# A graph propagation and a set-choosing LSTM on one core: the last propagation pass written out by row block, the first input weights fetched earlier

## The reference, cut to what matters

```python
# x: (1250, 512) float32; 21250 edges (src, dst, edge_weight)
def gnn(x, alpha, beta, sigma, edge_val, edge_row, edge_col, num_iters=10):
    xn = x * rsqrt(max(sum(x*x, axis=1, keepdims=True), 1e-12))
    sim_e = sum(xn[edge_row] * xn[edge_col], axis=-1)      # 0 on the diagonal
    sup = edge_val * exp(sim_e / (4 * exp(sigma)**2))
    denom = b + segment_sum(sup, edge_row)[:, None] * a + a   # a, b = exp(alpha), exp(beta)
    out = x
    for _ in range(num_iters):                              # 10 passes
        Ax = segment_sum(sup[:, None] * out[edge_col], edge_row)
        out = (x * b + (Ax + out) * a) / denom
    return out

def lstm(x, W_ih, W_hh, b_ih, b_hh, W_sel, b_sel):          # 4 weight sets, 1250 steps
    for t in range(1, T):
        logits = concat(h, c, x[t]) @ W_sel.T + b_sel
        s = argmax(logits)                                  # the set of this step
        g = x[t] @ W_ih[s].T + h @ W_hh[s].T + b_ih[s] + b_hh[s]
        h, c = lstm_activate(g, c)

x = x + gnn(layernorm(x))          # x1 in the kernel
return x + lstm(layernorm(x))      # y in the kernel is layernorm(x1)
```

## Time and profile before

| what | before |
|---|---|
| three executions, us | 6814.09, 6814.86, 6822.49 (median 6814.86) |
| the profiled execution, us | 6817.24 |
| its span, us | 6815.5 |
| granted TensorE clock, mean | 0.959 of full speed |
| busy: TensorE matmul / weight load | 6117.3 us (90%) / 4119.5 us (60%) |
| busy: VectorE / ScalarE / GpSimd | 3616.7 (53%) / 1805.4 (26%) / 1686.4 (25%) |

### The profile page before, as it was taken

How to read it: one execution, slowest core, us unless ns; L and a number is a source line. 1 busy time by engine, 2 the same in 40 slices (tenths; PEclk the granted TensorE clock), 3 DMA queues, 4 the chain that set the end, 5 groups by cost and what they waited for, 6 DMA issues and landing times.

```text
span 6815.5 us, 340711 instructions
## 1 busy us (share of the span) xinstructions
PE 6117.3 (90%) x126674; PEld 4119.5 (60%) x126675; DVE 3616.7 (53%) x19152; ACT 1805.4 (26%) x6561; POOL 1686.4 (25%) x4128
## 2 busy tenths in 40 slices
PE   6727999789999999999999999999999999999986
PEld 3523444666666666666666666666666666666663
DVE  5553111245565556555665555566556655556555
ACT  1001000522332223223332333233333333233321
POOL 4733111412222222222222222222222222222220
PEclk8758999589999999999999999999999999999999
DMA  3230000622222122122222222222222222222210
GB/s 95 1 77 0 0 0 0 192 71 58 62 63 58 57 60 65 55 60 60 65 63 60 62 61 60 60 63 63 61 60 65 64 61 63 59 63 62 61 52 27
DMA packets 691011, 389.94 MB, mean 57 GB/s; under 512 B 47835, under 2 KB 670811, under 8 KB 690720
## 3 DMA queue, kind: packets, MB, share of 16 engines
q1 hardware_dynamic: 659746, 369.66, 18.5%
q0 software_dynamic: 24192, 0.10, 1.1%
q10 hardware_dynamic: 7038, 19.69, 0.9%
HBM read 370.96 MB, written 18.38 MB: 57 GB/s over the span
## 4 chain that ended last, share of the span: by engine, by line
PE 70%; DVE 6%; issue 5%; DMA 1%; DVEq 0%; SPq 0%; ACT 0%; POOL 0%; POOLq 0%
PE ps L1016 33%; PE ps L1078 15%; PE ps L1025 8%; PE ps L1009 5%; PE ps L1005 4%; DVE hsum L843 2%; PE ps L1002 2%; PE ps L991 1%; DVE osum L851 1%; DVE acts L861 1%; DVE gates L848 1%; DVE osum L854 1%; DMA wring<-in_w_ih 1%; DVE cprod L857 0%; PE ps L978 0%
## 5 line engine op out<-in xcount | busy, mean ns | idle before, releaser
L1016 PE MATMUL ps<-WH,hparts 128*2 128x384 f16 x49760 | 2303.0, 326 | 196.6 <-issue 176.1
L1016 PEld LDWEIGHTS ps<-WH,hparts 128*2 128x2 f16 x49760 | 1053.4, 83 | 1044.7 <-issue 292.9
L843 DVE TRANSPOSE_TENSOR_REDUCE hsum<-ps 128x12 f32<-128x384 f32 x1250 | 728.7, 583 | 1793.0 <-PE ps L1016 1788.0
L1078 PE MATMUL ps<-xcur,wcur 128*128 128x64 f32 x9728 | 1341.9, 281 | 85.7 <-issue 12.4
L1078 PEld LDWEIGHTS ps<-xcur,wcur 128*128 128x128 f32 x9728 | 1178.5, 191 | 273.3 <-issue 210.2
L454 POOL COPY xT<-hfull 128x4 f32 x1250 | 239.5, 192 | 3727.2 <-DVE hfull L872 3727.2
L470 POOL COPY wcur<-wring 128x512 f32<-128x512 f32 x1216 | 743.4, 611 | 445.1 <-ACT gxb L598 443.3
L1025 PEld LDWEIGHTS ps<-WH,hparts 128*2 128x2 f16 x40000 | 603.7, 83 | 352.7 <-issue 314.9
L1025 PE MATMUL ps<-WH,hparts 128*2 128x128 f16 x40000 | 781.2, 219 | 7.5
L583 ACT ACTIVATE gx_now<-gxb 128x16 f32 x1250 | 269.7, 216 | 1782.2 <-DVE pick L837 1707.1
L969 PE MATMUL ps<-O,Adj 128*128 128x512 f16 x3000 | 650.3, 380 | 77.2 <-DVEq L748 77.2
(11 more groups left out here) (147 smaller groups left out, 4983.8 us busy)
## 6 DMA issues: line engine op xcount, KB each, us to landing
wring<-in_w_ih SPq DMA_DIRECT2D x1280, 256.0 KB, 2.9
gxb<-in_w_hh ACTq DMA_DIRECT2D x32, 512.0 KB, 5.6
adjacency<-Adj SPq DMA_DIRECT2D x2, 6400.5 KB, 24.7
Adj<-adjacency SPq DMA_DIRECT2D x10, 640.0 KB, 7.5
sim<-adjacency SPq DMA_DIRECT2D x10, 640.0 KB, 6.3
adjacency<-total,where_ POOLq DMA_INDIRECT x168
x_rows<-X SPq DMA_DIRECT2D x1, 2560.0 KB, 8.7
wring<-x_rows SPq DMA_DIRECT2D x10, 256.0 KB, 3.5
```

Of the source, the lines that this page charges most:

```text
L843: dve.tensor_reduce(hsum[:, :], gate_ps.rearrange("p (c q) -> p c q", q=32), AX.X, ALU.add, apply_transpose=True).then_inc(turned, 1)
L1016: last = nc.tensor.matmul(gate_ps[32 * j:32 * j + 2, :], hparts[:, k, :], WH[:, s * KC + k, part, j, 0:3 * P], start=(k == 0 and part == 0 ...
L1078: last = nc.tensor.matmul(unit_ps, wcur[:, k, :], xcur[:, k, :], start=(k == 0), stop=(k == KC - 1))
```

## The change

Five things are changed. (1) The tenth pass is taken out of the loops: VectorE updates X and takes the statistics of each row block as it arrives, after row block 7 (EARLY = 8) it also scales, roots and normalises blocks 0 to 7, and after block 9 the last two; ScalarE and GpSimd no longer split the tenth result. (2) Transposes go by group of four row blocks first and by piece k second, in both places where they are used. (3) `sim` is placed first in the graph's memory and `wring` first in the LSTM's, so that wring lies over sim. (4) SyncE fetches the first four slices when the matrix is finished (`m_ready`), and issues the write of the guessed sets behind the loads of the fourth group. (5) VectorE prepares biases and scales before the guessed sets, and TensorE does not wait for `lx_ready` any more.

```diff
         with ExitStack() as graph:
+            sim = sb("sim", [P, 2, NP], f32, graph)
             X = sb("X", [P, RT, D], f32, graph)
...
-            sim = sb("sim", [P, 2, NP], f32, graph)
...
+        wring = sb("wring", [P, SUB, KC, P], f32)
         WH = sb("WH", [P, S * KC, 2, 4, D], f16)
         gxb = sb("gxb", [P, 2 * TB, UNITS], f32)
-        wring = sb("wring", [P, SUB, KC, P], f32)
...
+        EARLY = 8
...
-            sp.wait_ge(x1_ready, 1)
-            sp.dma_start(x1_dram.rearrange("(t p) d -> p t d", p=P), X[:, :, :]).then_inc(x1_out, 16)
-            sp.wait_ge(lx_ready, 1)
-            sp.dma_start(pick_dram.rearrange("(t p) -> p t", p=P), pick_t[:, :], allow_slow_non_contiguous=True).then_inc(lx_out, 16)
-            sp.wait_ge(x1_out, 16)
-            sp.wait_ge(graph_free, 1)
...
+            sp.wait_ge(m_ready, RT)
+            for k in range(KC):
+                load_slice(sp.snap(0), 0, k)
+            sp.wait_ge(x1_ready, 1)
+            sp.dma_start(x1_dram.rearrange("(t p) d -> p t d", p=P), X[:, :, :]).then_inc(x1_out, 16)
+            for g in range(1, G):
+                for k in range(KC):
+                    if k < KC - 1:
+                        sp.wait_ge(wring_free, g * (KC - 1) + k + 1)
+                    else:
+                        sp.wait_ge(proj_mm, g * SUB + SUB)
+                    load_slice(sp.snap(0), g, k)
+            sp.wait_ge(lx_ready, 1)
+            sp.dma_start(pick_dram.rearrange("(t p) -> p t", p=P), pick_t[:, :], allow_slow_non_contiguous=True).then_inc(lx_out, 16)
+            with sp.Fori(1, S) as q:
-            with sp.Fori(0, S) as q:
...
-            with pool.Fori(0, ITERS // 2) as i:
+            with pool.Fori(0, ITERS // 2 - 1) as i:
...
+            for r in range(RT):
+                low_part(O_parts[0], r, (ITERS - 1) * RT + r + 1)
...
-            with act.Fori(0, ITERS // 2) as i:
+            with act.Fori(0, ITERS // 2 - 1) as i:
...
-            take_root(3)
+            for r in range(RT):
+                high_part(O_parts[0], r, (ITERS - 1) * RT + r + 1)
+            take_root(3, 0, EARLY)
+            take_root(4, EARLY, RT)
...
+            def finished_rows(r):
+                dve.wait_ge(t_ready, ITERS * RT + r + 1)
                 link(dve.scalar_tensor_tensor(out=X[:, r, :], in0=T[:, r, :], scalar=float(2.0 ** -OS), in1=X[:, r, :],
                                               op0=ALU.mult, op1=ALU.add))
+                link(dve.bn_stats(stats[:, r, :], X[:, r, :]))
+            def normalised_rows(first, end):
+                layernorm_scale(first, end)
+                for r in range(first, end):
+                    dve.tensor_scalar(O1[:, r, :], X[:, r, :], mv[:, r, 0:1], rstd[:, r:r + 1], ALU.subtract, ALU.mult).then_inc(y_ready, 1)
+            with dve.Fori(0, ITERS - 1) as i:
+                for r in range(RT):
+                    next_rows(r, dve.snap(i * RT + (r + 1)))
+            dve.wait_ge(t_low, ITERS * RT)
+            for r in range(RT):
+                next_rows(r, (ITERS - 1) * RT + r + 1)
+                finished_rows(r)
+                if r == EARLY - 1:
+                    normalised_rows(0, EARLY)
             dve.sem_inc(x1_ready, 1)
-            layernorm_stats()
...
+            normalised_rows(EARLY, RT)
...
-            def transposes(src, first, ready, want):
-                for k in range(KC):
-                    for q, (r0, m) in enumerate(TQ):
-                        i = first + k * len(TQ) + q
+            def transposes(src, first, ready, banks_free):
+                for q, (r0, m) in enumerate(TQ):
+                    if q == 1:
+                        banks_free()
+                    for k in range(KC):
+                        i = first + q * KC + k
...
-            transposes(O1, NTQ, y_ready, 0)
+            transposes(O1, NTQ, y_ready, lambda: pe.wait_ge(t_ready, (ITERS + 1) * RT))
...
-            pe.wait_ge(lx_ready, 1)
```

More of the change, by code:

```diff
@@ L314, in load_unit, with load_slice @@
                              ).then_inc(wring_in[u], 16)
-            with sp.Fori(0, S) as q:
+            def load_slice(q, g, k):
+                sp.dma_start(wring[:, k, :, :].rearrange("p u n -> p (u n)"),
+                             w_ih[:, bass.ds(q, 1), order[g], k * D:(k + 1) * D].rearrange("p a n -> p (a n)")
+                             ).then_inc(wring_in[k], 16)
+            sp.wait_ge(m_ready, RT)
[13 more added lines that the diff above has]
+            with sp.Fori(1, S) as q:
                 for g in range(G):
@@ L499, in _, with take_root @@
             act.activation(ab[:, 2:3], scal_b[:, 2:3], ACT.Exp, scale=-2.0).then_inc(ab_ready, 1)
-            def take_root(n):
+            def take_root(n, first=0, end=RT):
                 act.wait_ge(square_ready, n)
-                act.activation(root[:, :], square[:, :], ACT.Sqrt).then_inc(root_ready, 1)
+                act.activation(root[:, first:end], square[:, first:end], ACT.Sqrt).then_inc(root_ready, 1)
             take_root(1)
@@ L635, in _, with inverse_root @@
             roots = [0]
-            def inverse_root(to):
+            def inverse_root(to, first=0, end=RT):
+                to_c, root_c, newton_c, square_c = (one[:, first:end] for one in (to, root, newton, square))
                 roots[0] += 1
@@ L641, in inverse_root, with layernorm_scale @@
                 dve.wait_ge(root_ready, roots[0])
[L642 to L646, removed]
+                link(dve.reciprocal(to_c, root_c))
+                link(dve.tensor_tensor(newton_c, to_c, to_c, ALU.mult))
+                link(dve.tensor_tensor(newton_c, newton_c, square_c, ALU.mult))
+                link(dve.tensor_scalar(newton_c, newton_c, -0.5, 1.5, ALU.mult, ALU.add))
+                link(dve.tensor_tensor(to_c, to_c, newton_c, ALU.mult))
+            def layernorm_scale(first=0, end=RT):
+                for r in range(first, end):
+                    dve.bn_aggr(mv[:, r, :], stats[:, r, :]).then_inc(v, 1)
+                    chain[0] += 1
+                dve.wait_ge(v, chain[0])
+                link(dve.tensor_scalar(square[:, first:end], mv[:, first:end, 1], EPS, None, ALU.add))
+                inverse_root(rstd, first, end)
             def layernorm_stats():
@@ L652, in layernorm_stats @@
                 dve.wait_ge(v, chain[0])
[L653 to L658, removed]
+                layernorm_scale()
             dve.wait_ge(x_in, 32)
@@ L748, in _ @@
             dve.sem_inc(prop_ready, 1)
[L750 to L757, removed]
@@ L758, in _, with next_rows @@
-            for r in range(RT):
+            def next_rows(r, n):
+                dve.wait_ge(prop_mm, n)
+                dve.scalar_tensor_tensor(out=T[:, r, :], in0=ps[:, r % 8, :], scalar=float(2.0 ** -MS), in1=XB[:, r, :],
+                                         op0=ALU.mult, op1=ALU.add).then_inc(t_ready, 1)
+            def finished_rows(r):
+                dve.wait_ge(t_ready, ITERS * RT + r + 1)
                 link(dve.scalar_tensor_tensor(out=X[:, r, :], in0=T[:, r, :], scalar=float(2.0 ** -OS), in1=X[:, r, :],
```

27 lines of the change are left out of this document (11 added, 16 removed).

## The result

| what | before | changed |
|---|---|---|
| six executions each, median us | 6817.83 | 6786.39 (6782.36 to 6793.79) |
| the profiled execution, span, us | 6815.5 | 6783.0 |
| granted TensorE clock, mean | 0.959 | 0.962 |

What follows compares the result with a forecast made beforehand. TensorE bounds 70% of the span; what matters is the stretch from last propagation matmul to first LSTM step. -41.2 + 11.5 + 1.2 - 1.5 = -30.0 us gives 6787.2 profiled, 6784.8 against the median; range 6770 to 6797.

Steps and rivals of the forecast that it cites:

- its own signs: Prediction wrong if block 9's row is over 6.5 us late, fifth-group stall absent or over 14 us, or LSTM time changes.
- End of propagation: VectorE's early part ends before block 9 arrives, so no delay; X complete at 1210.0, last normalisations at 1212.7 us.
- Transposes to logits: Most transposes and copies run before the last normalisations; graph_free at 1214.2 us, logits start 22.8 us earlier.
- Logits: The 80 set-logit matmuls on TensorE stay unchanged at 15.8 us.
- Logits to projection: Biases prepared earlier save 4.6 us, first slices fetched early 13.8; projection starts at 1231.9 us.
- The words: Writing the guessed sets' 1280 words ahead of the fifth group's refills stalls TensorE there, costing 11.5 us, bounds 0 and 14.
- Sharing with the recurrent weights: Projection groups sharing DMA with recurrent-weight loads take 7.69 us; 1.2 us lost, bounds 0 and 4.
- First transposes: Early in the kernel, the new order waits for four blocks instead of ten: 1.5 us earlier, bounds 0 and 1.7.
- A (no stall): Rival: SyncE's refills in projection aren't held by the words; gain 41.5 us, time 6773; chance 0.13.
- B: Rival: moved SBUF places cost in every LSTM step; break-even 24 ns per step, 6847 us at 50 ns; chance 0.05.
- C (full clock in projection): Rival: TensorE stays at clock 1.0 through logits and projection; logits 8 us less, time 6762; chance 0.06.
- D (gain given back): Rival: words stall projection refills twice, or sharing costs 8.4 us a group; 17 us more, 6802; chance 0.05.

Runs made afterwards that it cites:

- order-only kernel: Kernel before with only the new order of the transposes, in both places: 6810.6 us, ratio 0.9996.
- places-only: Kernel before with only the new places in SBUF (sim first in the graph's memory, wring first in the LSTM's): 6818.5 us, ratio 1.0003.
- kept-busy kernel: Changed kernel with guessed sets as ten rows, ScalarE's second root behind four copies, and 12 and 8 extra TensorE matmuls during waits: 6747.2 us, ratio 0.9895.
- words-first kernel: Changed kernel with the guessed sets' words written first, then the first four slices fetched: 6792.1 us, ratio 0.9971.

## Why the prediction was right, point by point

By its own signs it passed narrowly. It put the one stall at the fifth group, where TensorE waited 1.4 us; the main wait, 4.4 us, was at the fourth. The time behind the first choice moved by 4.1 us, where "more than a few" was to count against it. And one slip in its bounds: with a stall of 14, sharing of 4 and no gain at the first transposes, 41.2 leaves 23.2 us, not 22.

**End of propagation.** Right: block 9 was not delayed, VectorE was free of the early part 2.75 us before it came, X left 2.2 us after the T row.

**Transposes to logits.** The step "`graph_free` comes at 1214.2", 6.45 us after the T row, failed by 1.75 us. I had checked that ScalarE's queue was idle where the root stands, but not what stands behind the root: twelve copies, of which eight could have run. With four copies ahead of the root the interval was 6.8 us. The transposes ran at a granted clock of 1.00, as TensorE's stretches in the changed kernel show:

```profile
1203.30:1206.30 3.00, 3.00 (x29) 1.00 0.00 0
1209.30:1210.80 1.50, 0.11 (x2) 0.76 1.04 388
...
1212.30:1228.30 16.00, 16.00 (x76) 0.50 0.67 217
```

The 29 matmuls of the first row are transposes alone. In the order-only kernel the clock also rose from 0.50 to 1.00 while nothing but transposes ran:

```profile
1227.00:1229.00 2.00, 2.00 (x11) 0.50 0.00 0
1229.00:1231.80 2.80, 2.80 (x22) 0.83 0.00 0
1231.80:1232.90 1.10, 0.02 (x1) 1.00 0.00 0
```

So what the Trainium skill ("TensorE: Matmul & The Clock Gate", Part 4: PE-mode transpose) says, that transposes don't count as activity for the full clock, does not hold here, and the 1 to 1.5 us that the prediction weighed for it were not paid.

**Logits.** Costed as unchanged, and 1.5 us longer than in the profile from before. That profile was the slowest of three with the old propagation: the logits took 13.8 us in the order-only kernel and 13.4 in the places-only one, but 17.3 in seven of the eleven profiles with the changed propagation. Against those two the loss is 3.5 to 4 us. The middle row above shows the clock falling in the idle stretch before them; before the change the transposes ran without a gap, ended 0.9 us ahead of them, and they began at full clock:

```profile
1237.00:1238.50 1.50, 1.48 (x14) 1.00 0.40 68
```

The last gap alone is not it: with the root behind six or four copies it was 0.74 us, and the logits still took 17.3. TensorE there also stood 1.8 or 1.4 us ahead of its last eight transposes. The kept-busy kernel filled both gaps and gained 3 us, so the idle time between the propagation and the logits is the cause; how much each gap costs was not tried.

**Logits to projection.** Right: 18.5 us, forecast 18.4. Of the 13.8 us put to the first slices, the kernel with the slices after the logits shows 5.8 for the fetch; the rest is put to the words, as the words-first kernel (13.6 us later behind the guess) bears out.

**The words.** The mechanism was right, the term mis-sized: 11.5 us taken, some 5.8 us of waits measured (7.1 over two groups, with ordinary sharing in it; 8.1 to 8.2 in the three other profiles with the words at this place and the first slices early). The price came from one execution with 18.6 us from the words to the slice; the order-only, places-only and words-first kernels gave 12.6 to 14.5, and in the changed kernel TensorE went on 9.95 us after the issue (1262.60 - 1252.65). It hit the fourth group, not the fifth. Doubling the words and writing them as rows show the cause.

**Sharing with the recurrent weights.** Groups away from the words took 6.8 to 7.7 us, and from 1316 us on all took 6.83; the forecast had sharing end at 1323.

**First transposes.** 1.1 us at the first edge matmul, 1.3 in the order-only kernel; forecast 1.5. The other 3.3 us of the first stretch aren't explained. The eleven profiles with the changed propagation have the T row between 1201.4 and 1206.2, the three with the old one at 1205.8, 1206.5 and 1207.75, so some of it is scatter and some may be real.

**LSTM.** Costed at nothing; 6.2 us were lost from the last group on: 2.1 before the first choice, 4.1 behind it. The first of these stretches took 5.3 us in four of the fourteen profiles, the one from before among them, and 6.6 to 8.5 in the others, the order-only (7.3) and places-only (7.7) kernels included, so it isn't the change's doing alone. Of the second the new places may be a part (above). Not settled.

**The rivals.** A (no stall) fell. B fell as a cost of 24 ns per step. C (full clock in projection) fell: the clock was 0.50 in the whole projection. D (gain given back) fell. Against the forecast, 1.7 (root), 1.5 (clock) and 6.2 us (behind the projection) were lost, 3.0 (first stretch) and 8.9 (projection) won: the total is right partly by cancellation.

## What to carry to other kernels

When a step is taken out of the way, read the whole queue of every engine that it touches: an instruction that waits costs what stands behind it, even where the engine was idle before. A small write in many pieces is not small: here 1280 words held up 256 KB loads until 10 us and more after their issue, wherever they stood on the queue, and turning them into ten rows took that away for 0.6 us. And a price from one execution of a DMA stall needs a second one.

## What had not been expected of the hardware

Idle stretches of 1 to 2 us ahead of slow small matmuls cost their clock too: keeping TensorE busy in both of them gave 3 us of 17.

The LSTM's pace moved with TensorE's instruction stream ahead of it, in which the LSTM has no part. First to last set choice took 5389 to 5399 us in the ten kernels whose TensorE stream is close to the old or the changed one, 5384 and 5386 in the two with one added transpose, 5363 with 20 more matmuls. Two rows of the page without, then with the extra work (busy, mean ns, idle before):

```profile
L1055 PE MATMUL ps<-WH,hparts 128*2 128x384 f16 x49760 | 2294.0, 326 | 193.3 <-issue 172.9
...
L1044 PE MATMUL ps<-wselT,acts 128*1 128x4 f32 x10000 | 436.8, 166 | 19.5 <-DVE acts L897 4.3
```

```profile
L1063 PE MATMUL ps<-WH,hparts 128*2 128x384 f16 x49760 | 2293.0, 326 | 181.8 <-issue 161.9
...
L1052 PE MATMUL ps<-wselT,acts 128*1 128x4 f32 x10000 | 428.3, 166 | 21.0 <-DVE acts L897 4.7
```

Each matmul takes the same; the idle time put to "issue" fell from 172.9 to 161.9 us, and the small products' sum from 436.8 to 428.3. The traces show where part of it lies. Of the 21.6 us between these two profiles, 9.2 fall in two single steps near the start, the times from one set choice to the next: 11.0 against 5.8 us in the third, 9.6 against 5.6 in the tenth. In the kernel without the extra work TensorE paused in each of them, put to "issue":

```profile
1374.22 2.73 PE L1055 MATMUL ps<-WH,hparts 128*2 128x384 f16 x32 [4.46 <-issue]
...
1410.42 1.28 PE L1117 MATMUL ps<-xcur,wcur 128*128 128x64 f32 x8 [3.99 <-issue]
```

Both kernels pause once in the first step (3.6 and 4.2 us); behind it TensorE has no pause of 1 us or more up to 1440 us with the extra work. In the 70 us from the first choice on, the DMA queue that carries instructions moved this without and then with it (packets, MB, share):

```profile
q8 instruction: 8, 0.13, 0.8%
```

```profile
q8 instruction: 3, 0.05, 0.4%
```

So these two pauses go together with the loading of instructions; whose they are, the trace does not say. The changed kernel has the first pause (4.5 us) and not the second. The other 12 us are spread over all the remaining steps. That TensorE's instructions lie at other addresses may be the reason for both. It was not tried; the cause stays open, and with it whether those 21 us can be had without the extra work.
